# A two-layer transformer block in one kernel: the last layer of the last two chunks done batch by batch, and the order of the steps laid anew

## The reference

```
x = x + 0.5 * FFN0(LN(x))      # silu(x w1) * (x w2), two 512x512 layers with gelu, down to 128
x = x + ATT0(LN(x))            # (theta phi^T) g / sqrt(128), no softmax
x = x + 0.5 * FFN0(LN(x))      # the same weights again
x = x + 0.5 * MOE(LN(x))       # gates from the first token of each batch, 2 of 8 experts
x = x + ATT1(LN(x))            # 16 heads of 8, rotary, causal softmax, output projection
x = x + 0.5 * MOE(LN(x))
```

## Time and profile before

| | |
|---|---|
| median of three runs | 692.27 us |
| profiled execution, its own time | 693.0 us |
| its span in the trace | 690.6 us |
| TensorE busy | 650.5 us, 94% (fillers included, L1017) |
| VectorE busy | 491.1 us, 71% |
| ScalarE busy | 495.8 us, 72% |
| GpSimd busy | 304.4 us, 44% |

### The profile page before, as it was taken

How to read it: one execution, slowest core, us unless ns; L and a number is a source line. 1 busy time by engine, 2 the same in 40 slices (tenths; PEclk the granted TensorE clock), 3 DMA queues, 4 the chain that set the end, 5 groups by cost and what they waited for, 6 DMA issues and landing times.

```text
span 690.6 us, 14730 instructions
## 1 busy us (share of the span) xinstructions
PE 650.5 (94%) x5536; PEld 492.9 (71%) x5536; DVE 491.1 (71%) x1278; ACT 495.8 (72%) x850; POOL 304.4 (44%) x473
## 2 busy tenths in 40 slices
PE   4999999999999999999999999889989999998996
PEld 3787878888887878877788877556555665565675
DVE  6667466577567686658786679989896788877341
ACT  5799688778777878877887685267756877566751
POOL 1402121232133262226474547568677554554643
PEclk9999999999999999999999999999999999999999
DMA  9200000000000011000020354215233311121001
GB/s 297 79 0 1 1 0 1 2 1 0 1 1 0 1 47 46 1 2 0 24 70 23 89 202 136 92 50 178 86 111 116 128 64 62 59 79 31 19 17 32
DMA packets 41624, 37.12 MB, mean 54 GB/s; under 512 B 2849, under 2 KB 36929, under 8 KB 41553
## 3 DMA queue, kind: packets, MB, share of 16 engines
q1 hardware_dynamic: 41552, 36.17, 16.8%
HBM read 21.21 MB, written 14.68 MB: 52 GB/s over the span
## 4 chain that ended last, share of the span: by engine, by line
PE 61%; DVE 17%; ACT 10%; issue 5%; DMA 3%; POOL 2%; SPq 1%; POOLq 0%; DVEq 0%; ACTq 0%
PE PSA L863 19%; PE PSA L867 18%; DVE MX L1189 6%; PE PSA L1047 5%; DMA QS<-dq 3%; DVE G L1111 3%; PE PSA L882 3%; PE PSA L1034 3%; PE PSA L999 2%; ACT PSA L1235 2%; PE PSA L977 2%; ACT G L1231 1%; PE PSA L984 1%; DVE ST L1082 1%; DVE RA L1182 1%
## 5 line engine op out<-in xcount | busy, mean ns | idle before, releaser
L1189 DVE TENSOR_REDUCE MX<-PSA 128x6 f32<-128x768 f32 x128 | 118.6, 950 | 25.2 <-PE PSA L1006 24.8
L863 PE MATMUL PSA<-ah,WH 128*128 128x512 f32 x320 | 129.9, 406 | 0.6 <-DVE G L1111 0.5
L867 PE MATMUL PSA<-al,WH 128*128 128x512 f32 x320 | 125.2, 391 | 0.0
L1235 ACT ACTIVATE PSA<-PSA,SC 128x512 f32<-128x512 f32 x128 | 84.7, 662 | 55.0 <-PE PSA L867 54.4
L1316 ACT ACTIVATE PB<-PSA 128x768 f32<-128x768 f32 x128 | 100.7, 815 | 13.6 <-PE PSA L1034 13.3
L863 PE MATMUL PSA<-bh,WH 128*128 128x512 f32 x256 | 104.8, 409 | 2.7 <-DVE G L1111 2.3
L1395 POOL TENSOR_SCALAR_AFFINE_SELECT PB<-PB 128x512 f32<-128x512 f32 x128 | 80.4, 635 | 53.8 <-ACT PB L1316 51.6
L867 PE MATMUL PSA<-bl,WH 128*128 128x512 f32 x256 | 100.2, 391 | 0.0
L1345 POOL TENSOR_SCALAR VE<-MV 128x4 f32<-128x4 f32 x48 | 11.3, 236 | 196.7 <-DVE MV L1086 196.7
L1116 DVE TENSOR_TENSOR al<-PSA,ah 128x512 fp32r<-128x512 f32 x64 | 44.0, 687 | 52.6 <-ACT ah L1242 52.2
L863 PEld LDWEIGHTS PSA<-ah,WH 128*128 128x128 f32 x320 | 60.2, 188 | 13.3 <-issue 0.7
(11 more groups left out here) (126 smaller groups left out, 1368.5 us busy)
## 6 DMA issues: line engine op xcount, KB each, us to landing
KS<-dk SPq DMA_DIRECT2D x32, 192.0 KB
QS<-dq SPq DMA_DIRECT2D x32, 192.0 KB
dk<-CB SPq DMA_DIRECT2D x16, 192.0 KB, 2.4
dq<-CB SPq DMA_DIRECT2D x16, 192.0 KB, 2.3
X<-in_x SPq DMA_DIRECT2D x8, 256.0 KB, 6.9
dk<-CB SPq DMA_DIRECT2D x16, 128.0 KB, 2.0
dq<-CB SPq DMA_DIRECT2D x16, 128.0 KB, 2.0
VA<-in_ones SPq DMA_DIRECT2D x4, 512.0 KB
```

The source lines that it names most:

```text
L863: e.matmul(o, WH[:, col:col + 128], hi, start=first, stop=False)
L867: return e.matmul(o, WH[:, col:col + 128], low, start=False, stop=last)
L1189: e.tensor_reduce(MX[:, u % 2, 1:4, :].rearrange("p t (l g) -> p l t g", l=2)[:, :, :, g], PSA[:, b:b + 2, 0:384].rearrange("p l (t k) -> ...
L1235: e.activation(bank(b), bank(b), ACT.Gelu, scale=SC[:, k:k + 1]).then_inc(a_gelu, 1)
```

## The change

1. **Half chunks at the end.** For chunks 6 and 7, `fin` runs a new job `half_moe` on each unit as soon as it is projected, and stores 128 KB at a time. Its steps: statistics of two tiles and the added epsilon on VectorE, `pow` on GpSimd, normalisation on VectorE, two transposes, a ScalarE copy of 256 columns, one logit row, maximum, difference and indices on VectorE, tanh on ScalarE; then `half_pick` on VectorE, which loads two indices in registers, forms the two gates and the expert matrix in two operations; `half_expert` and its sum.
2. **The picks of chunk 5** (and of the other whole chunks from NC - 3 on, of which there is only this one) are laid only after all pass2 steps.
3. **Six more banks** go to the ring `sr` once the last pass2 is laid.
4. **No fillers before the flag's branch**: `fill` asks for `self.opened`.
5. **Planner numbers**: some durations in TAKES, a duration of 2.7 us for each of the first three "up" steps, QUEUED 0.8, LEAD 16, `lead()` 5.95 and 6.1, `attend` 6, `maxima` 1.0, and (1, 0) three places later in QUEUE.

```diff
-QUEUED = 1.0
-LEAD = 12
+QUEUED = 0.8
+LEAD = 16
...
-QUEUE = [(0, 0), (0, 1), (0, 2), (0, 3), (0, 4), (1, 0), (0, 5), (0, 6), (0, 7),
+QUEUE = [(0, 0), (0, 1), (0, 2), (0, 3), (0, 4), (0, 5), (0, 6), (0, 7), (1, 0),
...
+        if name == "up" and not self.opened:
+            late = "up_first"
...
-        if not free or not self.count.get("up"):
+        if not free or not self.opened:
...
+        while kind == "n" and c >= NC - 3 and self.turn["probs"] < NB:
+            yield
         wb = self.put("pick", c=c, i=n, src=gt, given=lg)
...
-            self.add(2.5, self.attend(2 * c + h, a, va))
+            self.add(6, self.attend(2 * c + h, a, va))
...
-        return 5.5 if self.count.get("pass1", 0) < self.count.get("pass2", 0) + LEAD else 6.5
+        return 5.95 if self.count.get("pass1", 0) < self.count.get("pass2", 0) + LEAD else 6.1
...
-        self.add(5.2, self.maxima(u, p1))
+        self.add(1.0, self.maxima(u, p1))
...
+        if u == NB - 1:
+
+            for b in range(6):
+                self.sr.ids.append(b)
+                self.sr.free[b] = self.bank[b]
...
-        if self.outs[u // 2] == 2:
+        if u // 2 >= NC - 2:
+
+            o = yield from self.half_moe(u, o)
+            yield from self.until(o.done)
+            self.put("half_store", c=u // 2, u=u)
+        elif self.outs[u // 2] == 2:
...
+                elif st.name == "half_stat":
...
+                    for j in range(2):
+                        t = e.bn_stats(ST[:, i, j, :], X[:, 2 * u + j, :])
...
+                    e.tensor_scalar(VE[:, i, 0:2], MV[:, i, 0:2, 1], EPS, None, ALU.add).then_inc(v_half_ve, 1)
+                elif st.name == "half_norm":
+                    w.wait_ge(g_half_rs, n + 1)
+                    for j in range(2):
+                        t = e.tensor_scalar(XN[:, i, j, :], X[:, 2 * u + j, :], MV[:, i, j, 0:1], RS[:, i, j:j + 1],
+                                            ALU.subtract, ALU.mult)
...
+                elif st.name == "half_pick":
+                    w.wait_ge(v_half_who, n + 1)
+                    w.wait_ge(v_table, 2)
+                    who = nc.values_load_multi_w_load_instructions(
+                        WHO[0:1, i, 0, 0:2], (mybir.EngineType.DVE,), min_val=0, max_val=7)[1]
+                    w.wait_ge(a_half_tanh, n + 1)
...
+                    e.tensor_scalar(WB[:, i, 0, :], PT[:, bass.ds(who[0], 1), :].rearrange("p o d -> p (o d)"),
+                                    GS[:, i, 0, 0:1], None, ALU.mult).then_inc(v_half_one, 1)
...
+                elif st.name == "half_power":
...
+                    e.tensor_tensor(RS[:, i, 0:2], VE[:, i, 0:2], MHALF[:, 0:2], ALU.pow).then_inc(g_half_rs, 1)
...
+                elif st.name == "half_store":
+                    w.wait_ge(v_x, ages[id(st)])
+                    e.dma_start(xout[:, 2 * u:2 * u + 2, :], X[:, 2 * u:2 * u + 2, :]).then_inc(s_out, 16)
```

More of the change, by code:

```diff
@@ L620, in fin, with half_moe @@
             self.put("store", c=u // 2)
+    def half_moe(self, u, src):
+        c = u // 2
+        yield from self.until(src.done - 0.5)
+        i, free = yield from self.lnr.get(self)
+        st = self.put("half_stat", c=c, u=u, i=i, emptied=free, src=src)
+        yield from self.until(st.done - 0.3)
+        st = self.put("half_power", c=c, u=u, i=i, src=st)
+        yield from self.until(st.done - 0.3)
+        st = self.put("half_norm", c=c, u=u, i=i, src=st)
+        yield from self.until(st.done)
+        x, xfree = yield from self.xtr.get(self)
+        b, free = yield from self.sr.get(self)
+        xt = self.put("half_xt", c=c, u=u, i=i, x=x, b=b, emptied=free, emptied2=xfree, src=st)
+        self.lnr.free[i] = self.sr.free[b] = [xt]
+        yield from self.until(xt.done)
+        n, nfree = yield from self.moer.get(self)
+        b, free = yield from self.sr.get(self)
+        lg = self.put("half_logit", c=c, u=u, x=x, i=n, b=b, emptied=free, emptied2=nfree, src=xt)
+        self.sr.free[b] = [lg]
+        yield from self.until(lg.done - 0.3)
+        gt = self.put("half_tanh", c=c, u=u, i=n, src=lg)
+        yield from self.until(gt.done - 0.3)
+        pk = self.put("half_pick", c=c, u=u, i=n, src=gt, given=lg)
+        yield from self.until(pk.done)
+        b, free = yield from self.sr.get(self)
+        o = self.put("half_expert", c=c, u=u, i=n, x=x, b=b, emptied=free, src=pk)
+        self.sr.free[b] = self.xtr.free[x] = self.moer.free[n] = [o]
+        return o
     def lay(self):
@@ L793, in build @@
             ages[id(st)] = x_age.get(st.c, 0)
-            if st.name in ("back", "att0", "expert", "proj"):
+            if st.name in ("back", "att0", "expert", "proj", "half_expert"):
                 k += 1
@@ L815, in emptied @@
                     w.wait_ge(a_y, m)
-                elif st.name in ("back", "att0", "expert", "proj"):
+                elif st.name in ("back", "att0", "expert", "proj", "half_expert"):
                     w.wait_ge(v_x, nth_x[id(st)])
+                elif st.name == "half_xt":
+                    w.wait_ge(a_half_xt, m)
+                elif st.name == "half_logit":
+                    w.wait_ge(v_half_who, m)
                 elif st.name == "flag":
@@ L964, in tensor @@
                     t.then_inc(p_logit, 1)
+                elif st.name == "half_xt":
+                    w.wait_ge(v_half_xn, n + 1)
+                    emptied(w, st.emptied)
+                    for j in range(2):
+                        t = e.transpose(PSA[:, b, 128 * j:128 * j + 128], XN[:, st.i, j, :], IDN[:, :])
+                    t.then_inc(p_half_xt, 1)
+                elif st.name == "half_logit":
+                    w.wait_ge(a_half_xt, n + 1)
+                    emptied(w, st.emptied)
+                    e.matmul(PSA[:, b, 0:8], XT[:, st.x, 0:1].to_broadcast([128, 128]), WR[:, :], start=True,
+                             stop=True).then_inc(p_half_logit, 1)
+                elif st.name == "half_expert":
+                    w.wait_ge(v_half_wb, n + 1)
+                    emptied(w, st.emptied)
+                    for k in range(2):
+                        t = e.matmul(PSA[:, b, 128 * k:128 * k + 128], XT[:, st.x, 128 * k:128 * k + 128],
+                                     WB[:, st.i, 1, :], start=True, stop=True)
+                    t.then_inc(p_half_expert, 1)
                 elif st.name == "table":
@@ L1161, in vector @@
                     for s in st.emptied2:
-                        w.wait_ge(p_expert, s.n + 1)
+                        w.wait_ge({"expert": p_expert, "half_expert": p_half_expert}[s.name], s.n + 1)
                     for h in range(2):
@@ L1259, in scalar @@
                     for s in st.emptied2:
-                        w.wait_ge({"att0": p_att0, "expert": p_expert}[s.name], s.n + 1)
+                        w.wait_ge({"att0": p_att0, "expert": p_expert, "half_expert": p_half_expert}[s.name], s.n + 1)
                     e.activation(XT[:, st.x, :], bank(b), ACT.Copy).then_inc(a_xt, 1)
+                elif st.name == "half_xt":
+                    w.wait_ge(p_half_xt, n + 1)
+                    for s in st.emptied2:
+                        w.wait_ge({"expert": p_expert, "half_expert": p_half_expert}[s.name], s.n + 1)
+                    e.activation(XT[:, st.x, 0:256], PSA[:, b, 0:256], ACT.Copy).then_inc(a_half_xt, 1)
+                elif st.name == "half_tanh":
+                    w.wait_ge(v_half_df, n + 1)
+                    e.activation(TT[:, i, 0:1], DF[:, i, 0:1], ACT.Tanh, scale=0.5).then_inc(a_half_tanh, 1)
                 elif st.name == "fuse":
@@ L1347, in gpsimd @@
                     e.tensor_tensor(RS[:, i, :], VE[:, i, :], MHALF[:, :], ALU.pow).then_inc(g_rs, 1)
+                elif st.name == "half_power":
+                    w.wait_ge(g_c, 2)
+                    w.wait_ge(v_half_ve, n + 1)
+                    e.tensor_tensor(RS[:, i, 0:2], VE[:, i, 0:2], MHALF[:, 0:2], ALU.pow).then_inc(g_half_rs, 1)
                 elif st.name == "norm":
```

44 lines of the change are left out of this document (42 added, 2 removed), and 25 rows, old and new, of the table TAKES.

## The result

The changed kernel takes **695.99 us** (median of 5 runs, 695.26 to 698.9), the kernel before 692.44 beside it (5 runs, 691.38 to 692.83): a ratio of 1.0064, 95% interval 1.0043 to 1.0085. By the medians it is 3.6 us slower (3.0 to 5.9 by the interval), where 10.5 us faster was forecast. A ratio here takes in every run and can differ by a few tenths of a per cent from that of the two medians, so differences of medians are good to about 1 us. The profiled execution took 695.26 us with a span of 693.5, so on the profile's own scale the change costs 2.3 us (693.0 before).

The account below looks back on a forecast made before the run. TensorE was taken to bound the FFN stage, with 39.5 us open in attention and a tail of waiting steps; gains 7.3 + 2.1 + 1.1 + 0 = 10.5 us off the profiled 693.0 gave 682.5, so median 681.8, range 676 to 688.

Parts of the forecast that it names:

- The queue, the priorities, the durations: FFN and attention stages: the edits only permute needed work, so 0 us, with 4 us to either side.
- (1, 0) three chunks later: FFN stage: one chunk's MOE and rotary work moves about 75 us down, well before first use; TensorE's sum stays.
- theory M: Follow-up runs' theory, not the prediction's: preparation pushed behind the last FFN matmul costs the start of the attention stage.
- The half chunks: Chain after the last projection: 11.2 us instead of 18.5, a gain of 7.3 us.
- for such meetings: Tail: 0.6 us added for two half-chunk chains meeting in VectorE's queue, none at best, 2.5 at worst.
- The picks of chunk 5 and the banks: End of attention: masks follow exponentials directly, the last weigh ends earlier with six more banks; a gain of 2.1 us.
- The flag: Kernel start: without 30 fillers the first gated product starts 1.4 us earlier; gain 1.1 us, between 1.4 and -0.6.
- B: Tail: half chunks block each other on VectorE, or picks precede powers on GpSimd; 685.8 to 690.9 us, chance 0.12.
- C: Attention stage: reloc comes late, the middle loses 12 us, 694 us; chance 0.10 with other middle costs over 9 us.
- A: Attention stage: the new order finds 4 to 8 us of open time, 674 to 677.8 us; chance 0.15 with better.

Follow-up runs that it names:

- struct_old_order: The change with the old queue, priorities and durations, so only half chunks, held picks, six banks and no fillers before the flag: 687.07 us, 0.9928.
- flag_alone: The kernel before with no fillers before the flag's branch, nothing else: 692.18 us, 1.0001.
- power_before_picks: struct_old_order with chunk 5's picks laid only after the fourth half power, and 2.6 us for half_pick in the planner: 686.78 us, 0.9926.
- change_fill_09: The whole change with FILLED 0.9 instead of 0.65, same step order with more fillers between: 694.68 us, 1.0033.

## Why the prediction was wrong

**The queue, the priorities, the durations (0, within 4 us): the step that failed.** It read: "None of these edits removes needed work; each only permutes it, and TensorE was needed for 200.6 of the 240 us." The stage grew by 12.8 us, for a shift of the last exponential by 9.4. In the medians the structural edits alone gain 5.1 us and the whole change loses 3.6, so the new order costs 8.7 us where 0, within 4, had been put. Of the 14.1 us between forecast and result these are the larger part; the other 5.4 are those of the structural terms below, and with them alone the time would have been 687.1, inside the range. Three things were wrong in that sentence. A permutation need not be free when it carries work over the border between a stage bound by TensorE and one paced by VectorE: the earlier trace rows had VectorE's 190.62 of 240 us beside TensorE's column, and only TensorE's was used. How much of the 8.7 us this is stays open; theory M, which priced it alone, missed. The 4 us to either side were a guess at the size of a new order's scatter; ten nanoseconds in the table move the time by 3.8 and 4.5 us, the one to three places in the queue by 7 to 15. And the scatter was taken to be even on both sides. Of the eleven kernels in which queue, durations or priorities are new, none has its last exponential as early as before (663.8 to 680.2, against 662.1). That the old order is a good one among its neighbours is shown by these; why no neighbour found is better is not.

"(1, 0) three chunks later ... still inside the full FFN stage" looked at the step itself and not at what follows from it. Six `qk` steps stand ahead of the FFN's last matmul in the new list, eight in the old.

**The half chunks (7.3 us).** The chain after the last projection is 14.1 us in the changed kernel and 15.3 in struct_old_order, not 11.2; and the way to it got longer. Singly the prices held or were too high: the power took 0.70 us against 1.05, the loads 0.73 in the last pick against 1.0, the store some 2.5 (691.02 to 693.5) against 2.8. What was mis-sized are the 0.6 us "for such meetings", bounded above by 2.5: with the three prices put right the rest of the sum is 9.7, so the meetings took some 4.4 us in the changed kernel (an estimate), as picks, sums and transposes of three half chunks stand in one row of orders, 3.3 us from one to the next. Besides, 2.7 of the 18.5 us were GpSimd's wait for chunk 6, which the held picks alone remove; the prediction credited them to the half chunks. Net of both, the half chunks are worth about zero (1.1 and 0.3 us slower by the bare medians).

**The picks of chunk 5 and the banks (2.1 us).** They are worth 5.7 us with the fill condition, all of struct_old_order's gain and more: 1.5 us for the picks, 4.2 for the banks. The way to the last projection is 3.7 us shorter with both (6.3 for 10.0), where 2.1 had been put, and the chain after it 2.4 us shorter (16.1 for 18.5), which this term did not count. The prediction gave the banks one clause ("six banks more mean that it no longer waits for one to be emptied") and no price.

**The flag (1.1 us).** The trace does what was said (the changed kernel's timeline; it answers to the earlier trace rows):

```profile
18.34 0.19 PE L978 MATMUL PSA<-FS,FL 128*1 128x1 f32 x2 [1.45 <-DVE FL L1225]
...
18.57 0.15 DVE L1228 CAST FI<-PSA 1x1 int32<-1x1 f32 x1 [0.28 <-PE PSA L978]
...
19.76 1.49 PE L1093 MATMUL PSA<-IDN 128*128 128x128 f32 x11 [1.23 <-issue]
19.98 1.41 DVE L1187 SCALAR_TENSOR_TENSOR G<-PSA,SC,G 128x512 f32<-128x512 f32 x2 [1.27 <-ACT G L1357]
```

The flag's matmul was forecast for 18.4 and came at 18.34, the gated product for 19.9 and came at 19.98. The later steps of the FFN stand 1.3 us earlier too. Yet flag_alone's median is that of the kernel before (1.0001, 0.9989 to 1.0012). What happened to the 1.3 us on the way from the FFN to the median isn't settled; flag_alone's one profiled execution, with a span of 688.5, was also the shortest of its ten runs (690.95 us), and that of the kernel before (693.0) lies 0.9 to 1.6 us above that kernel's medians beside the experiments. It is a warning for the tables above: one execution against another is good to a us or two, not to tenths.

**The rivals.** B was right in the first half of its mechanism (the half chunks block each other on VectorE; power_before_picks speaks against the second, the picks ahead of the powers) and stands inside the tail, where 6.5 us were won all the same. C named the right stage and nearly the right time, 694, for the wrong reason. Idle time before the first matmuls of pass1, the answer to the earlier trace rows:

```profile
  DVE MX L1315: 14.7, 28
  DMA QS<-dq: 3.9, 4
```

Landings end 3.9 us of it in 4 waits, less than the 5.5 in 6 before: `reloc` isn't late. VectorE's maxima end 14.7. A did not occur. The range left out what lies above 688 with 0.11, and it came out at 696; a term that said "0, within 4" without a row for the 4 should have widened it.

## What to carry over

Where a planner lays the whole order, a change of its inputs is a new draw: measure first by how much a meaningless change (10 ns in one duration) moves the time, keep that as the error of every "it only permutes", and keep a structural edit on the old order until it has been measured there. When work is moved over the border of two stages, look at the engine that paces the second one too, not only at the one that bounds the first. Ablate bundled edits both ways, alone and left out: here the durations were +10.4 us alone and -4.7 in the bundle (by the medians), and the one part that paid (held picks and six banks, 5.7 us) was hidden in it.

## What the runs showed of the hardware

- TensorE's granted clock fell to 0.50 at 441 us with TensorE in thin use (2.02 and 1.56 us of work in two stretches of 3 us, the longest gap 1.59 us); in change_fill_09, with 2.58 and 2.18 us of work there and a gap of 1.31, it stayed at 1.00. Trainium skill, TensorE: Matmul & The Clock Gate, HAM oscillation: an idle gap can return the array to half rate. The trace agrees for the gap at 441. At the flag the same kernel has gaps of 1.45 and 1.23 us and its granted clock stays at 1.00; the next FFN matmuls follow at a pitch of 0.23 us, the upper level.
- The float32 matmuls of an expert took 1.22 us at the lower level (444.08) and 0.60 at the upper (421.00), for the same four shapes.
- Two register loads on VectorE took 1.4 us in the first half pick (672.78 to 674.17) and 0.73 in the last. The prediction's estimate by the Trainium skill, Advanced Engine Details and Errata, Clock Domains, was 1.25 us, from 1.0 on GpSimd's sequencer; the trace has less than either in the last half pick.
- `pow` on GpSimd took 0.70 us on two columns and 1.04 on four, so its cost is not fixed as the prediction had taken it.
